# A two-layer graph attention kernel: the proof's count behind two row tiles, pieces searched during scoring, low halves moved to POOL, first requests reordered

## The reference, cut to what matters

```python
# layer 0: dense attention of 4096 rows, biased by twice the adjacency matrix (N = 4096, D = 512)
q = x @ Wq.T + bq;  k = x @ Wk.T + bk;  v = x @ Wv.T + bv
a = q @ k.T / sqrt(D) + adj + adj
x1 = layernorm(x + softmax(a) @ v)
# layer 1: attention over neighbours, 8 heads of 64
feats = einsum('nf,hfd->hnd', x1, W)
dense = leaky_relu(e_self[:, :, None] + e_neigh[:, None, :], 0.2) + (-1e10 * (1.0 - adj))[None]
out = relu(concat_heads(softmax(dense) @ feats + b))
return layernorm(x1 + out)
```

## Time and profile before

| | |
|---|---|
| median of 3 runs (range) | 1744.04 us (1743.17 to 1746.19) |
| the profiled execution | 1742.32 us, of which the span of the core is 1740.5 us |
| PE busy | 1572.2 us (90% of the span) |
| DVE busy | 1265.2 us (73%) |
| POOL busy | 830.6 us (48%) |
| ACT busy | 536.3 us (31%) |
| mean granted PE clock | 0.962 of 2.4 GHz |

### The profile page before, as it was taken

How to read it: one execution, slowest core, us unless ns; L and a number is a source line. 1 busy time by engine, 2 the same in 40 slices (tenths; PEclk the granted TensorE clock), 3 DMA queues, 4 the chain that set the end, 5 groups by cost and what they waited for, 6 DMA issues and landing times.

```text
span 1740.5 us, 27963 instructions
## 1 busy us (share of the span) xinstructions
PE 1572.2 (90%) x10052; PEld 971.9 (56%) x10052; DVE 1265.2 (73%) x2492; ACT 536.3 (31%) x794; POOL 830.6 (48%) x787
## 2 busy tenths in 40 slices
PE   8989888999999999999999999999999999885910
PEld 3434467666666666666666666666666666432400
DVE  5888666768875886688768866887688668877454
ACT  4545400222232223222322232223222332343225
POOL 2866400446554555454545454545455545434151
PEclk9999999999999999999999999999999999998865
DMA  7366767568766876687569766975697568675057
GB/s 260 131 242 235 273 225 237 188 213 278 236 206 194 303 254 200 207 302 251 197 195 314 247 195 198 311 249 194 203 306 255 190 211 270 224 253 200 25 158 252
DMA packets 188316, 395.11 MB, mean 227 GB/s; under 512 B 20624, under 2 KB 26768, under 8 KB 187024
## 3 DMA queue, kind: packets, MB, share of 16 engines
q1 hardware_dynamic: 183056, 376.52, 65.1%
q0 software_dynamic: 5120, 16.78, 3.0%
HBM read 335.55 MB, written 57.67 MB: 226 GB/s over the span
## 4 chain that ended last, share of the span: by engine, by line
PE 77%; DVE 11%; DMA 4%; ACT 3%; issue 2%; SPq 1%; POOL 1%; another core or an unknown queue 0%; DVEq 0%; ACTq 0%; POOLq 0%
PE O L826 34%; PE S L785 30%; PE X L742 4%; PE O L742 3%; PE S L742 3%; DMA ring<-in_adjT 2%; PE O L785 2%; DVE big L1182 1%; DVE ring L1399 1%; DVE work L1357 1%; PE X L867 1%; ACT ring L1145 1%; DVE ring L1322 1%; DVE cand L1295 1%; DVE vring L1217 1%
## 5 line engine op out<-in xcount | busy, mean ns | idle before, releaser
L826 PE MATMUL O<-vring,ring 128*128 128x512 f16 x2928 | 708.6, 380 | 11.8 <-DVE ring L1399 9.5
L785 PE MATMUL S<-yb,big 128*128 128x256 f16 x4998 | 625.0, 273 | 12.2 <-DVE ring L1331 11.0
L785 PEld LDWEIGHTS S<-yb,big 128*128 128x128 f16 x4998 | 486.4, 98 | 164.8 <-DVE ring L1331 15.0
L698 POOL TENSOR_TENSOR ring<-work,ring 128x512 f16<-128x512 f32 x222 | 265.1, 1194 | 607.0 <-ACT ring L1002 607.0
L826 PEld LDWEIGHTS O<-vring,ring 128*128 128x128 f16 x2928 | 286.2, 98 | 271.0 <-issue 16.8
L1117 ACT ACTIVATE work<-ring 128x512 f32<-128x512 f32 x256 | 160.8, 628 | 796.7 <-DVE ring L1322 764.2
L708 POOL TENSOR_TENSOR work<-work 128x512 f32<-128x512 f32 x248 | 344.6, 1390 | 58.0 <-ACT work L1117 56.8
L1331 DVE TENSOR_TENSOR ring<-S,ring 128x256 f32<-128x256 f32 x476 | 199.8, 420 | 230.4 <-PE S L785 228.5
L1357 DVE TENSOR_TENSOR work<-work,ring 128x512 f32<-128x512 f32 x248 | 215.8, 870 | 0.7
L1336 DVE TENSOR_TENSOR ring<-S,ring 128x256 f32<-128x256 f32 x357 | 150.6, 422 | 56.9 <-PE S L785 50.7
L1322 DVE TENSOR_TENSOR ring<-BC,ring 128x512 f32<-128x512 f32 x256 | 173.9, 680 | 0.6 <-PE BC L852 0.6
(11 more groups left out here) (136 smaller groups left out, 1047.9 us busy)
## 6 DMA issues: line engine op xcount, KB each, us to landing
ring<-in_adjT SPq DMA_DIRECT2D x256, 256.0 KB, 4.3
big<-x_scratch SPq DMA_DIRECT2D x128, 512.0 KB, 6.3
big<-in_adj SPq DMA_DIRECT2D x256, 256.0 KB
vring<-v_scratch SPq DMA_DIRECT2D x244, 256.0 KB, 3.9
yb<-y_scratch SPq DMA_DIRECT2D x56, 256.0 KB, 5.9
y_scratch<-yb SPq DMA_DIRECT2D x7, 1792.0 KB, 9.1
ring<-in_xT SPq DMA_DIRECT2D x8, 1024.0 KB, 7.2
v_scratch<-vring SPq DMA_DIRECT2D x32, 256.0 KB, 2.4
```

The source lines that it names most:

```text
L698: pool.tensor_tensor(ring16[:, e % SLOTS, 1, :], pf[:, e % NPF, :], ring16[:, e % SLOTS, 0, :], ALU.subtract).then_inc(lo_done, 1)
L785: mm = pe.matmul(bank, keys_of(p, keys, a, c), yb[:, b % 2, queries, m, c, :], start=(start and c + a + m == 0), stop=(c == 1 and a == 1), ...
L826: mm = pe.matmul(O[j][:, :], ring16[:, e % SLOTS, a, j * P:(j + 1) * P], values_of(e)[:, m, :], start=(k + a + m == 0), stop=(k == NT - 1 ...
```

## The change

Six edits. (1) `piece_load` gives 2 pieces instead of 1 to the steps with `s` mod 16 = 2, 6, 7 and 8, and none to steps 128 to 139, so that the search ends in step 126. (2) `LO_FIRST` goes from 222 to 236 (`NC - 20`): the low halves of elements 222 to 235 are made on POOL. (3) In the loop over the last elements, `subtract(e)` stands ahead of `last_lo(e - 1)`; the last `find` moves to step 129 and `prove_single` to step 135. (4) PE's count of the proof moves from ahead of the last 12 elements to behind the matmuls of query tiles 0 and 1, into another bank, and the flag is written at the very end of DVE's program. (5) In the first 18 steps SP requests four chunks and two pairs of keys in each even step and none in odd steps, and loads query parts two steps later. (6) At the end of preparation SP stores two value tiles ahead of the first two pairs, and ACT runs `queries(7)` ahead of the last two `value_hi`; `hi_count` gives the counts for the new order.

```diff
@@ piece_load
-            if LAG <= s < NCP:
-                return 1 if 2 <= s % NP <= 8 else 3
-            return 2 if NCP <= s < NCP + 12 else 0
+            if not LAG <= s < NCP:
+                return 0
+            return 1 if 3 <= s % NP <= 5 else 2 if s % NP in (2, 6, 7, 8) else 3
@@
+        def hi_count(g, n):
+            return {(NB - 2, 2): 3 * NB - 1, (NB - 1, 0): 3 * NB - 3, (NB - 1, 1): 3 * NB - 2}.get((g, n), 3 * g + n + 1)
@@
-        LO_FIRST = 2 * (NCP - LAG + 1)
+        LO_FIRST = NC - 20
@@ SP, last group of preparation
-                    for p in range(2):
-                        load_pair(p)
                 for kt in range(g * JB, (g + 1) * JB):
                     if kt % JB == 2 and g + 1 < NB:
                         store_x(g + 1)
+                    elif kt % JB == 2:
+                        load_pair(0)
+                        load_pair(1)
@@ SP, steps
                 if s < LAG:
-                    for c in range(min(2 * s + 4, SLOTS), min(2 * s + 6, SLOTS)):
+
+                    for c in range(min(2 * s + 4, SLOTS), min(2 * s + 8, SLOTS)) if s % 2 == 0 else ():
                         load_adj(c)
...
                 if s + NX + 1 < LAG:
-                    load_pair(s + NX + 1)
+                    if s % 2 == 0:
+                        load_pair(s + NX + 1)
+                        load_pair(s + NX + 2)
...
-                if s == 6:
+                if s == 8:
                     sp.wait_ge(y_out[1], 16 * (NB // 2))
-                if 6 <= s < 13:
-                    load_y_part(1, s - 6)
+                if 8 <= s < 15:
+                    load_y_part(1, s - 8)
@@ PE, end
-            pe.wait_ge(ok_chain, 9)
-            pe.wait_ge(chain_read, 4 * NCP)
-            pe.matmul(S[0][0:1, 0:1], okw[:, 0:1], ones[:, 0:1], start=True, stop=True).then_inc(sums_ready, 1)
...
             for e in range(NC - TAIL, NC):
                 values(e, 1)
-            pe.wait_ge(flag_set, 1)
+            pe.wait_ge(ok_chain, 9)
+            pe.matmul(BC[0:1, 0:1], okw[:, 0:1], ones[:, 0:1], start=True, stop=True).then_inc(sums_ready, 1)
             transpose_x1(J0)
@@ ACT, preparation
+                if g == NB - 1:
+                    queries(g)
                 value_hi(g * JB + 2)
                 value_hi(g * JB + 3)
...
-                queries(g)
+                if g < NB - 1:
+                    queries(g)
@@ DVE, end
+                if s == NCP + 1:
+                    find(NT - 1)
+                if s == NCP + 7:
+                    prove_single()
             for e in range(2 * (STEPS - TAIL // 2 - LAG + 1), NC):
+                subtract(e)
                 last_lo(e - 1)
-                subtract(e)
-                if e == NC - 4:
-                    find(NT - 1)
-                    prove_single()
             last_lo(NC - 1)
...
-            dve.wait_ge(sums_ready, 2)
-            dve.tensor_copy(flag[:, :], S[0][0:1, 0:1]).then_inc(flag_set, 1)
...
             last_norm()
+            dve.wait_ge(sums_ready, 2)
+            dve.tensor_copy(flag[:, :], BC[0:1, 0:1]).then_inc(flag_set, 1)
```

10 lines of the change are left out of this document (5 added, 5 removed).

## The result

The changed kernel takes 1695.6 us in the median of four runs (1693.7 to 1698.8), the kernel before 1743.6 us in four on the same chip (1742.8 to 1746.2): the ratio is 0.9724, with a 95% interval of 0.9706 to 0.9742. I had forecast 1706, 1697 to 1719. The direction was right; the time lies 1.4 us outside the range. The profiled execution took 1695.5 us, with a span of 1693.7.

The account below looks back on a forecast made before the run. It took PE as busy in the middle, with gains only where PE waits for chunks (first 18 pairs) and DVE's proof (tail). -13.9 + 1.8 + 0.5 - 27.1 + 1.0 = -37.7 us: 1704.6 profiled, 1706 median, range 1697 to 1719.

Parts of the forecast that it names:

- First 18 pairs, the requests: Start of scoring: earlier chunk requests end DVE's waits, PE gains 10.7 us plus 3.2 us of clock: -13.9 us.
- First 18 pairs, ACT's order: Start of scoring: `queries(7)` moved ahead makes DVE's first read 2.6 us later, four reads in a row return 0.8: +1.8 us.
- The middle: Steps between start and tail: 24 more pieces, 16.3 us on DVE, mostly covered by its idle time: +0.5 us.
- Steps 128 to 135: Tail's start: DVE loses pieces and 14 low halves, POOL gets the halves; tile 27's transposes come 6.3 us earlier.
- Elements 236 to 255: Last elements: 1.85 us each instead of 3.16; gain 27.1 us including steps 128 to 135, and +1 us for PE's clock.
- The proof: Tail: PE's 24.2 us wait for the proof's last DVE instruction goes; PE waits some 5 us for DVE instead.
- The end: From PE's last row sums on: all stays as before, 0, at most +1 us.
- (d): Rival, tail: DVE's halves fall between the sums, PE is the bound in tile 0, gain 33 not 27: 1699; chance 0.1.
- (a): Rival, start: the requests don't help, chunks queue or the store delays them; 13.9 shrinks to 2 to 5: 1716; chance 0.15.
- (b): Rival: the tail is slower, tile 27 no earlier, 6 us, and elements at 1.95 us: 1714; chance 0.15.
- (c): Rival, middle: the added pieces delay reads, costing half to all of 16.3 us: 1714 to 1722; chance 0.08.
- (e): Rival, middle: second pieces delay chain products and PE's clock falls, 56 us in 28 steps: 1762, slower; chance 0.03.

Follow-up runs that it names:

- a_old_act: The changed kernel with ACT's `queries(7)` behind the last two `value_hi` again, as before: 1683.2 us, ratio 0.9701 to the kernel before.
- b_requests: The kernel before with only SP's part of the change, the new order of requests: 1717.1 us, ratio 0.9897.
- a_old_requests: The changed kernel with SP's requests in the old order: 1701.3 us, ratio 0.9808 to the kernel before.
- a_again: The changed kernel itself, unaltered, on another chip: 1688.0 us, ratio 0.9732 to the kernel before.
- b_pieces: The kernel before with only the new `piece_load` and `pieces_at`: 1714.5 us, ratio 0.9883.
- a_lo222: The changed kernel with DVE making the low halves from element 222 instead of 236, as before: 1691.5 us, ratio 0.9752 to the kernel before.
- a_late_proof: The changed kernel with the last `find` and the proof on DVE at element 252 again: 1687.1 us, ratio 0.9730 to the kernel before.
- a_no_sums: The changed kernel with POOL's last 19 sums one column wide, output wrong, for timing alone: ratio 0.9700 to the kernel before.
- a_half_first: The changed kernel with, for the last ten elements, the low half ahead of the next subtraction again: 1704.8 us, ratio 0.9832 to the kernel before.
- a_scale_first: The changed kernel with POOL's scale of a row tile ahead of the gather in the same step: ratio 0.9739 to the kernel before.
- best2: The changed kernel with ACT's old order, earlier query parts, later `find`, POOL's scale between halves from step 128, and PE's last matmuls reordered: ratio 0.9633 to the kernel before.
- b_ kernels: Runs of the kernel before with one part of the change each; ratios 0.9883 to 0.9979.
- a_ kernels: Runs of the changed kernel with one thing altered each; ratios to the kernel before 0.9700 to 0.9832.
- a_old_count: The changed kernel with PE's count ahead of the last twelve elements and the flag's copy amid DVE's last evictions, as before: 1685.4 us, ratio 0.9716 to the kernel before.

## Why the prediction was right or wrong, step by step

**First 18 pairs, the requests** (-13.9, bounds 0 and -14): the mechanism was right, the size too small and its bound false. The requests are worth -17.4 us on the kernel before and -15.7 on the changed one, each from one trace with the old requests, where A spreads over 2.7 us. I counted PE's waits for chunks and missed that the two first pairs' requests also hold up a store. The row was in my own group: ACT's `value_hi` with 9.50 us idle, released by the store of values. I used that row for its time and not for its wait.

**First 18 pairs, ACT's order** (+1.8, bounds 0 and +3): mis-sized, it measured +5.5. Two steps failed. First, I compared the read with that of before (209.9). With the new requests alone it comes at 205.4 to 205.5 (a_old_act, b_requests), because `value_hi` no longer waits so long for the store; with `queries(7)` ahead it waits for PE's last product instead. Second, I left the 6.4 us from the last `value_hi` to the read unchanged. They became 8.6 (the same in a_old_requests, and 6.4 in a_old_act and b_requests), because moving `queries(7)` forward lets POOL's sums of the queries start sooner, and they now run beside the low halves on DVE that the read stands behind. The timeline before:

```profile
207.47 1.82 DVE L1182 SCALAR_TENSOR_TENSOR big<-xr,big 128x768 f16<-128x768 f32 x2
...
209.21 0.68 DVE L1182 SCALAR_TENSOR_TENSOR ring<-xr,ring 128x512 f16<-128x512 f32 x1
```

And in the changed kernel, with POOL's sum between them:

```profile
208.09 2.89 DVE L1190 SCALAR_TENSOR_TENSOR big<-xr,big 128x768 f16<-128x768 f32 x2
...
210.13 1.97 POOL L665 TENSOR_TENSOR work<-work 128x512 f32<-128x512 f32 x1
...
210.90 1.74 DVE L1190 SCALAR_TENSOR_TENSOR ring<-xr,ring 128x512 f16<-128x512 f32 x1
```

Counted from PE's first product of scores the read comes 12.2 us later instead of 3.3: 6.8 us by the later `value_hi` and 2.1 by this path. Of these 8.9 us 3.4 came back, four reads in a row being the part that I had counted at 0.8. That the read came within 0.2 us of the forecast is luck: the last `value_hi` ended at 204.05 and not at 206.0, in a trace whose scoring began 1.6 us sooner than before, and the path was 2.2 us too short. In a_again the read of the same kernel comes at 214.0. The two errors of this stretch (requests and ACT) cancelled to 0.1 us, so its agreement is no proof of its terms.

**The middle** (+0.5, bounds 0 and 16.3): the sign was wrong, and this is the step that failed most. "There only a new stall can change the time, and nothing can be won": PE's idle time could be won, and was in part: in B it fell from 15.1 to 11.7 us. I left out a gain by added work, because I looked at totals of DVE's idle time and never at the waits that PE had there.

**Steps 128 to 135** (-6.3, bounds 0 and -10): measured -7.9, with two errors in it. The transposes of tile 24 came 4.2 us sooner (28.0 instead of 32.2 us behind the last maxima) and not 5.3: PE waits 3.4 us for a low half on POOL in step 130, and the six matmuls behind that wait, which I had put at 1.3 us, take 2.72 us, because the granted clock was 0.50 there, the level of 1.2 GHz. The three steps to tile 27 took 25.0 us and not 27.4: POOL was expected at 9.1 us a step and took 8.76, PE 8.2 to 8.4. By b_pieces the pieces that are gone give 6.3 us, by a_lo222 the halves on POOL 2.5, and the `find` in step 129 costs 1.0 (a_late_proof).

**Elements 236 to 255** (pace 1.85 us; -20.8 in this stretch, + 1.0 for the clock): measured -24.2 at 1.68 us. The pace was the sum of POOL's 1.27 us and DVE's half at 0.6, one strictly after the other; a_no_sums shows that they do hold each other up, and the timeline that 0.2 us overlap. The 18 elements took 30.5 us instead of 33.3, which is 2.8 of the 3.4 us that this term missed; the first of them came 0.6 us sooner behind the transposes. The clock didn't fall: 1.00 in the 20 us above and, by the same view, in the 40 us behind them, so the +1.0 was nothing. PE, which I expected to wait 5 us, waited 3.8. The Trainium skill, SBUF — State Buffer, Who interferes with whom, says that a VectorE instruction with two SBUF inputs and a GpSimd instruction that reads SBUF lock each other out. In the middle the traces agree: with POOL ahead, DVE's `maximum` of 0.68 us ends 0.55 us behind POOL's half. In the tail they agree but for the 0.2 us.

**The proof** (PE's longest wait, 24.2 us): its removal was hardly a gain of its own. The wait measured how late DVE was, and b_pieces, a_half_first and a_late_proof show what made it late: pieces and order, 16.3 and 15.3 us.

**The end** (0, at most +1): measured +3.0, for the most part not by the change. See below.

Together the errors are: middle -4.7, tile 27 -1.6, elements and clock -4.4, first product -1.6, end +3.0, start +0.1: -9.1 us (rounded), from 1704.6 to 1695.5. The first product and the end, which the change did not make, hid 1.4 us of the miss. Of the rivals, (d) had PE as the bound of tile 0, 1699; that was nearest in time, but by luck, since DVE stayed the bound. (a), (b), (c) and (e) did not occur. My range had no room below for a gain in the middle.

## What to carry to other kernels

Where VectorE and GpSimd hold each other up, an extra instruction can make a kernel faster by moving a neighbour 0.2 us out of the way: look at the durations of the same instruction in each block, not at their mean. A long wait names the engine that is late, not the work that makes it late; take that work away piece by piece before you credit the move of the waiting instruction. When a change moves two parts of one chain, price the second against the trace as the first would leave it. And an instruction that moves forward lets what waits for it start sooner too: ask beside what that will then run.

## What the hardware did that I had not expected

DVE stands still in its last 60 us where the trace names nothing that the program waits for ("remote"), in the profiled runs of four kernels: in the first pair of runs, and in a_scale_first and best2, which ran on one chip. The same instruction in the timelines of three kernels, first in the changed kernel:

```profile
1656.84 0.17 DVE L1572 SCALAR_TENSOR_TENSOR yb<-yb 128x8 f32<-128x8 f32 x1 [7.01 <-remote]
```

In a_scale_first:

```profile
1659.33 0.17 DVE L1572 SCALAR_TENSOR_TENSOR yb<-yb 128x8 f32<-128x8 f32 x1 [5.54 <-remote]
```

In a_again, the changed kernel on another chip:

```profile
1663.71 0.17 DVE L1572 SCALAR_TENSOR_TENSOR yb<-yb 128x8 f32<-128x8 f32 x1
```

The kernel before has such a stop of 4.9 us at the same instruction. The stretch E is 115.9 and 118.9 us with it (118.6 in a_scale_first), and 107.5 to 111.2 in the traces of the other chips, where the kernel before took 1734.5 to 1735.1 us instead of 1740.4 and 1743.6 (best2, with a stop of 4.2 us, has a shorter program there). What DVE waits for there, and why on some chips only, stays open; I did not test it. The changed kernel has a second stop, of 2.1 us, so its stops are 4.2 us longer than those of the kernel before, and that covers the 3.0 us of E in the first pair of traces. That the change costs nothing there is not shown to better than about 1 us: without stops E is 107.5 to 109.4 us in the four b_ kernels and 108.1 to 111.2 in the a_ kernels; a_old_count, with the flag in its old place, has 108.1, a_again 109.6.
